# A logits bank that holds one place of the key tiles for four heads, instead of four key tiles of one head

## The chip, the cores and the metric

The kernel runs on one core of a Trainium2 chip. Its time is the device time of one execution in microseconds (us), given as the median of three runs.

## What is computed

Two blocks over an input `x` of 8 batches, 1024 tokens and 256 features, in fp32. The part that matters is the attention of the first block, with 16 heads of 16 features and a relative position term:

```
x = L0_attn_x
logits = einsum('bhqd,bhkd->bhqk', q, k) + einsum('bhqd,qkd->bhqk', q, embK[idx])
w = softmax(logits, axis=-1)
out = einsum('bhqk,bhkd->bhqd', w, v) + einsum('bhqk,qkd->bhqd', w, embV[idx])
x = x + layernorm(out @ Wo.T + bo)
x = x + layernorm(layernorm(x) @ ternary(W).T * alpha + bias)
```

`idx` is the distance of key and query, clipped to 64 on either side. So the relative term differs from token to token only in a band around the diagonal, and is one constant per side elsewhere.

## The kernel before

**Steps.** The heads are in two groups of 8 and the queries in tiles of 128. That makes 8 x 2 x 8 = 128 steps `s`. A step is worked in two halves (`blk` 0 and 1, four heads each), and four steps make a quad, of which there are 32. The 8 key tiles of a query tile are sorted by `near_first`: places 0 and 1 are the two that the band touches (left and right), places 2 to 7 lie further round.

**The stages of a step.** `row_max` forms the scores of one head in the two PSUM banks of `scores` (L748 on TensorE); VectorE adds the band to the first bank and takes its maximum (L1044), then takes the maximum of the second bank (L1047). TensorE may write the next head's first bank after L1044 has read it, and its second bank after L1047. `max_rows` turns the maxima. `weights` forms the logits transposed, in one of `NLOG` = 2 banks `logitsT` (L770); for places 0 and 1 a second matmul in transpose mode adds the band (L775). ScalarE takes the exponential of the whole bank into SBUF (L1251). `weighted` multiplies by the values into `oacc` (L800). `merge` joins left and right weights on VectorE (L1069). Once in a quad `relative` multiplies the merged weights of four steps by the table of the relative values (L812), and `relative_sum` and `out_norm` finish them. The projections of the next batch and the "tail" (output projection, the layer norms, the ternary matmul; L864) are spread between these.

**The banks of `weights`.** A half has eight banks: four of kind X (places 0 to 3), one for each head, and four of kind Y (places 4 to 7), one for each head. So an X bank takes six matmuls, four L770 and two L775, and a Y bank four L770. The bank that is used alternates, and each waits until ScalarE is done with the bank two before it: `pe.wait_ge(exp_ready, block + 1 - NLOG)`.

**Where the weights lie.** `wxr` in SBUF holds places 0 and 1 of four steps (`wx`) and, behind them, places 2 and 3 of one half (`wr`); one ACTIVATE writes to both. `wy` holds places 4 to 7 of one half.

**Order.** Each engine runs its stages in an order that a table of slots sets (`timetable`, with `LAG`): the X banks of a half stand at `o + 0.4 * j`, the Y banks at `o + 1.7 + 0.4 * j`, the heads of `row_max` at every 0.87 slots, `weighted` X at `o + 2.3`. The engines meet only at semaphores.

Below, a bank is called by its step's number in the quad, its half and its place in the half's eight banks: "X0 to X3" and "Y0 to Y3".

Of the kernel before, what the change touches and what calls it, by code (L numbers as in the profile page):

```python
# [14 lines left out]
P = 128  # L15
B, S, H = 8, 1024, 256
NH, D, MRP = 16, 16, 64
VOCAB = 2 * MRP + 1
T = S // P
G = 2  # L20
HG = NH // G
# [7 lines left out]
FAR = MAXROW + 2  # L29
ROWS = FAR + 3  # L30
# [3 lines left out]
WIN = 2 * P  # L34
# [3 lines left out]
QUAD = 4  # L38
# [3 lines left out]
QRING, BRING, VRING = 5, 7, 3  # L42
HB = HG // 2
# [266 lines left out]
def build(nc, a, out):  # L310
    with ExitStack() as ctx:
        def sb(name, shape, dt=F32):
            return ctx.enter_context(nc.sbuf_tensor(name, shape, dt))
# [12 lines left out]
        ident = sb("ident", [P, P])  # L326
# [14 lines left out]
        qs = [sb(f"qs{i}", [ROWS, HG, P], BF16) for i in range(QRING)]  # L341
        vs = [sb(f"vs{i}", [P, 2, T, HG, VW]) for i in range(VRING)]
        bands = sb("bands", [P, (BRING * HB + 1) * WIN])
        band = [bands[:, i * HB * WIN:(i + 1) * HB * WIN].rearrange("p (h c) -> p h c", h=HB) for i in range(BRING)]
        zeros = bands[:, BRING * HB * WIN:]
        praw = sb("praw", [P, HG, WIN])
        embk6, partmask = praw[0:SPLIT, 0, 0:VOCAB], praw[0:SPLIT, 0, VOCAB:VOCAB + 3]
        wxr = sb("wxr", [P, (QUAD * HG + 4) * WIN])
        wx = wxr[:, 0:QUAD * HG * WIN].rearrange("p (i h c) -> p i h c", i=QUAD, h=HG)
        wr = wxr[:, QUAD * HG * WIN:].rearrange("p (j c) -> p j c", j=4)  # L350
        wy = sb("wy", [P, 4, 512])
        junk = sb("junk", [P, 2, WIN], BF16)
        maxes = [sb(f"maxes{i}", [P, HG, 2]) for i in range(2)]
# [6 lines left out]
        x0 = wxr[:, 0:T * H].rearrange("p (t h) -> p t h", t=T)  # L360
        xc = sb("xc", [P, CHUNK, H])
        xnT = sb("xnT", [P, 2, CT])
        qf = sb("qf", [P, G, CT])
# [24 lines left out]
        value = counts(orders)  # L388
# [32 lines left out]
        def n(signal, stage, *k):  # L421
            return value.get((signal, stage) + k, 0)
# [35 lines left out]
        def wait_x1(eng, b, t):  # L458
            if last_tile(b, t):
                eng.wait_ge(x1_ended, t - T + QUAD + 1)  # L460
            else:
                eng.wait_ge(x1_ready, b * T + t + 1)

        def wait_praw(eng):

# [209 lines left out]
        def tensor_program(e):  # L675
            pe, order = Engine(e), orders["PE"]
            for stage, k in order:
# [80 lines left out]
                elif stage == "weights":  # L758
                    s, h, kind = k
                    m_, t = s // T, tile_of(s)  # L760
                    i, kk = s % QRING, ks[m_ % 2]
                    tiles = near_first(t)[0:4] if kind == "X" else near_first(t)[4:]
                    block = n("logits_ready", "weights", s, h, kind) - 1
                    lt = logitsT[block % NLOG]
                    pe.wait_ge(nm_in[s % 2], 32 * (s // 2 + 1))
                    pe.wait_ge(exp_ready, block + 1 - NLOG)
                    for c, kt in enumerate(tiles):
                        near = kind == "X" and c < 2
                        depth = ROWS if is_right(t, kt) else FAR
                        mm = e.matmul(lt[:, c * P:(c + 1) * P], kk[0:depth, h, kt * P:(kt + 1) * P], qs[i][0:depth, h, :],  # L770
                                      start=True, stop=not near, skip_group_check=True)
                        if near:
                            v = 2 * s + h // HB
                            pe.wait_ge(band_in[v % BRING], band_loads(v))
                            mm = e.matmul(lt[:, c * P:(c + 1) * P], band[v % BRING][:, h % HB, c * P:(c + 1) * P], ident[:],  # L775
                                          start=False, stop=True, is_transpose=True, skip_group_check=True)
                    mm.then_inc(logits_ready, 1)
                elif stage == "weighted":
# [11 lines left out]
                    for c, kt in enumerate(tiles):  # L790
                        for q0, q1, right in value_sides(t, kt):
                            for j in range(4):
                                h = 4 * blk + j
                                if kind == "Y":
                                    src = wy[:, j, c * P + q0:c * P + q1]
                                elif c < 2:
                                    src = wx[:, s % QUAD, h, c * P + q0:c * P + q1]
                                else:
                                    src = wr[:, j, (c - 2) * P + q0:(c - 2) * P + q1]
                                mm = e.matmul(oacc[32 * j:32 * j + VW, o0 + q0:o0 + q1], vs[m_ % VRING][:, int(right), kt, h, :],  # L800
                                              src, start=first and c == 0, stop=True, skip_group_check=True)
                    mm.then_inc(pvX if kind == "X" else pvY, 1)
                elif stage == "relative":
# [4 lines left out]
                    for i in range(8 * part + 2 * piece, 8 * part + 2 * piece + 2):  # L808
                        o0 = i % 8 * QUAD * HG * 2
                        for j in range(4):  # L810
                            q = 32 * j + 2 * i
                            mm = e.matmul(m[32 * j:32 * j + 32, o0:o0 + QUAD * HG * 2],  # L812
                                          reltab[:, 126 - q:128 - q, :].rearrange("p n d -> p (n d)"),
                                          wx[:, :, :, P + q:P + q + 2], start=True, stop=True, skip_group_check=True)
                    if piece == 3:
                        mm.then_inc(rel_summed, 1)
                elif stage == "relative_sum":
# [92 lines left out]
        def vector_program(e):  # L910
# [45 lines left out]
            for stage, k in order:  # L956
# [104 lines left out]
                    e.tensor_tensor(nm[:, 1], m[0:HG, 0:P], nm[:, 0], ALU.subtract).then_inc(nm_ready, 1)  # L1061
                elif stage == "merge":
                    s, blk = k
                    left, right = (wx[:, s % QUAD, HB * blk:HB * blk + HB, x:x + P] for x in (0, P))
# [111 lines left out]
        def scalar_program(e):  # L1176
            act, order = Engine(e), orders["ACT"]
            for stage, k in order:
# [41 lines left out]
                elif stage == "band_raw":  # L1220
                    s, blk = k
                    act.wait_ge(raw_summed, n("raw_summed", "band_raw", s, blk))
                    v = 2 * s + blk
                    if s:
                        act.wait_ge(band_out[(v - 2) % 4], 16 * ((v - 2) // 4 + 1))
                    dst, src = praw[:, HB * blk:HB * blk + HB, :], m[:].rearrange("p (h c) -> p h c", h=HB)
                    e.activation(dst[:, :, 0:P], src, ACT.Copy)  # L1227
                    e.activation(dst[:, :, P:WIN], src[:, :, P - 1:P].broadcast_to([P, HB, P]), ACT.Copy).then_inc(praw_ready, 1)  # L1228
                elif stage == "weights":
                    s, h, kind = k  # L1230
                    block = n("logits_ready", "weights", s, h, kind) - 1
                    lt = logitsT[block % NLOG]
                    act.wait_ge(logits_ready, block + 1)
                    done = pvX if kind == "X" else pvY
                    if kind == "X":
                        if s >= QUAD:
                            act.wait_ge(rel_summed, 2 * (s // QUAD))
                            act.wait_ge(pvX, value["pvX", s - QUAD, h // 4])
                        at_ = (s % QUAD * HG + h) * WIN
                        dst = bass.AP(wxr, at_, [[(QUAD * HG + 4) * WIN, P], [(QUAD * HG + h % 4) * WIN - at_, 2], [1, WIN]])  # L1240
                        src = lt[:].rearrange("p (a c) -> p a c", a=2)
                    else:
                        dst, src = wy[:, h % 4, :], lt[:]
                        for c in (1, 3):
                            act.wait_ge(q_out[0][c], 96)
                            act.wait_ge(k_out[0][c], 96)
# [144 lines left out]
```

## Time and profile before

| | |
|---|---|
| time, median of 3 runs | 2637.41 us (2637.28 to 2637.48) |
| span of the profiled execution | 2629.6 us (first to last instruction) |
| the runs' median less that span | 7.8 us |
| TensorE busy | 2474.5 us, 94% |
| VectorE busy | 2044.9 us, 78% |
| ScalarE busy | 1552.6 us, 59% |
| GpSimd busy | 926.1 us, 35% |
| mean granted TensorE clock | 0.984 |

The profiled execution's time outside of its span is not recorded; the three runs agree within 0.2 us, so the median stands for it. TensorE's busy share counts each matmul from its start to its modelled end, and neighbours overlap. The pace at which it gets through its work is therefore read from the starts in the timeline, and a wait from the note in brackets behind a row. The middle of the kernel is periodic: a quad takes about 79 us.

### The profile page before, as it was taken

The page shows a single profiled execution, that of the slowest core. Times are in us where ns is not written, and L with a number is a line of the kernel's source. Part 1 is how long each engine was busy: PE and PEld are TensorE (multiplying, and loading weights), DVE is VectorE, ACT ScalarE, POOL GpSimd, SP SyncE. Part 2 cuts the span into 40 slices and gives each one's busy share as a digit, 9 for nine tenths or more (in the row PEclk, how much of TensorE's full clock was granted, in tenths as well). Part 3 has the DMA queues.
Part 4 walks back from the last instruction along what each step waited for, and adds up shares of the span by engine and source line. Part 5 has one row for each costly group of instructions (what it writes and reads, how often), then busy time and mean ns, then how long its engine had stood idle before and what let it go on. Part 6 is the DMA issues. An engine that isn't in the chain of part 4 may idle for free.

```text
span 2629.6 us, 99990 instructions
## 1 busy us (share of the span) xinstructions
PE 2474.5 (94%) x41858; PEld 1901.8 (72%) x41858; DVE 2044.9 (78%) x5306; ACT 1552.6 (59%) x2993; POOL 926.1 (35%) x2211
## 2 busy tenths in 40 slices
PE   5699999999999999999999999999999999999995
PEld 3377777777777777777777777777777777777774
DVE  5577678876888768876788767987678876887786
ACT  3366666565666556665566665566666565666652
POOL 3002534335332443424434253433434334342014
PEclk9699999999999999999999999999999999999997
DMA  6655664557545565455645566445654556545410
GB/s 167 205 159 152 186 174 130 153 156 201 152 149 153 156 183 157 138 161 171 184 137 156 153 179 185 134 140 161 200 165 131 152 155 195 163 137 169 128 54 30
DMA packets 605183, 408.07 MB, mean 155 GB/s; under 512 B 149563, under 2 KB 604475, under 8 KB 604603
## 3 DMA queue, kind: packets, MB, share of 16 engines
q1 hardware_dynamic: 604730, 401.67, 52.8%
q8 instruction: 329, 5.39, 0.9%
q14 instruction: 124, 1.01, 0.1%
HBM read 205.95 MB, written 194.92 MB: 152 GB/s over the span
## 4 chain that ended last, share of the span: by engine, by line
PE 64%; DVE 23%; issue 6%; ACT 2%; SPq 2%; DMA 1%; POOL 1%; DVEq 0%; ACTq 0%; POOLq 0%
PE oacc L800 15%; PE logitsT L770 14%; PE scores L748 12%; DVE maxes L1047 9%; DVE junk L1044 8%; PE logitsT L775 7%; PE misc L705 4%; PE misc L864 3%; ACT wxr L1251 2%; PE misc L722 2%; DVE stats L922 2%; PE misc L825 2%; PE misc L812 1%; PE misc L732 1%; PE misc L850 1%
## 5 line engine op out<-in xcount | busy, mean ns | idle before, releaser
L770 PE MATMUL logitsT<-qs,ks 98*128 98x128 bf16 (+1 forms) x8192 | 977.5, 220 | 15.9 <-ACT wxr L1251 7.9
L1044 DVE CUSTOM_DVE_ANT_1 junk<-scores,bands 128x512 bf16<-128x512 f32 x988 | 678.2, 686 | 338.8 <-PE scores L748 295.3
L1251 ACT ACTIVATE wxr<-logitsT 128x512 f32<-128x512 f32 x1024 | 587.9, 603 | 453.4 <-PE logitsT L770 356.0
L770 PEld LDWEIGHTS logitsT<-qs,ks 98*128 98x128 bf16 (+1 forms) x8192 | 669.1, 99 | 192.0 <-issue 58.1
L1251 ACT ACTIVATE wy<-logitsT 128x512 f32<-128x512 f32 x1024 | 587.3, 597 | 307.5 <-PE logitsT L770 295.2
L748 PE MATMUL scores<-ks,qs 96*128 96x256 bf16 (+6 forms) x3712 | 686.8, 288 | 83.8 <-DVE maxes L1047 38.4
L1047 DVE TENSOR_REDUCE maxes<-scores 128x1 f32<-128x512 f32 x1024 | 701.3, 685 | 1.5 <-PE scores L748 1.5
L748 PEld LDWEIGHTS scores<-ks,qs 96*128 96x128 bf16 (+1 forms) x3712 | 285.1, 98 | 261.8 <-DVE maxes L1047 133.8
L775 PE MATMUL logitsT<-ident,bands 128*128 128x128 f32 x2048 | 463.3, 278 | 0.0
L1280 POOL TENSOR_SCALAR rs<-rs 128x1 int32<-128x1 int32 (+1 forms) x217 | 47.7, 220 | 897.3 <-DVE rs L927 888.2
L775 PEld LDWEIGHTS logitsT<-ident,bands 128*128 128x128 f32 x2048 | 291.7, 142 | 43.5
L1285 POOL TENSOR_SCALAR rs<-rs 128x1 f32<-128x1 f32 x744 | 274.1, 371 | 64.9
L800 PE MATMUL oacc<-wy,vs 128*17 128x128 f32 (+1 forms) x9216 | 274.1, 262 | 0.7 <-ACT wy L1251 0.7
L800 PE MATMUL oacc<-wxr,vs 128*17 128x128 f32 (+1 forms) x9216 | 274.1, 262 | 0.0
L800 PEld LDWEIGHTS oacc<-wy,vs 128*17 128x17 f32 x9216 | 205.7, 97 | 39.5 <-issue 19.9
L800 PEld LDWEIGHTS oacc<-wxr,vs 128*17 128x17 f32 x9216 | 205.7, 97 | 35.6 <-issue 13.6
L1290 POOL TENSOR_SCALAR rs<-rs 128x1 f32<-128x1 f32 x744 | 207.6, 282 | 66.1
L1227 ACT ACTIVATE praw<-misc 128x512 f32<-128x512 f32 x256 | 153.4, 599 | 44.3 <-DMA bs<-praw 39.9
L1069 DVE COPY_PREDICATED wxr<-later,wxr 128x512 f32<-128x512 int32 x224 | 172.2, 769 | 8.2 <-PE oacc L800 8.2
L1228 ACT ACTIVATE praw<-misc 128x512 f32<-128x512 f32 x256 | 156.4, 611 | 0.0
L812 PE MATMUL misc<-wxr,reltab 128*32 128x64 f32 x4096 | 102.7, 242 | 0.0
L732 PE MATMUL misc<-bandtab,qs 96*128 96x128 bf16 x1024 | 100.2, 220 | 0.2
(141 smaller groups left out, 2433.9 us busy)
## 6 DMA issues: line engine op xcount, KB each, us to landing
bs<-praw SPq DMA_DIRECT2D x256, 512.0 KB, 4.3
bands<-bs SPq DMA_DIRECT2D x224, 512.0 KB, 4.6
ks<-kd SPq DMA_DIRECT2D x64, 384.0 KB, 4.4
qs<-qd SPq DMA_DIRECT2D x112, 192.0 KB
bands<-bs SPq DMA_DIRECT2D x128, 128.0 KB, 3.3
qd<-qparts SPq DMA_DIRECT2D x60, 192.0 KB, 2.9
kd<-kparts SPq DMA_DIRECT2D x60, 192.0 KB, 2.6
qd<-qparts SPq DMA_DIRECT2D x60, 128.0 KB, 2.6
```

What stands on the lines that cost most here:

```text
L748: mm = e.matmul(scores[:, c:c + length], qs[i][0:depth, h, :], kk[0:depth, h, key:key + length], start=True, stop=True, skip_group_check=True)
L770: mm = e.matmul(lt[:, c * P:(c + 1) * P], kk[0:depth, h, kt * P:(kt + 1) * P], qs[i][0:depth, h, :], start=True, stop=not near, skip_group ...
L775: mm = e.matmul(lt[:, c * P:(c + 1) * P], band[v % BRING][:, h % HB, c * P:(c + 1) * P], ident[:], start=False, stop=True, is_transpose=Tr ...
L800: mm = e.matmul(oacc[32 * j:32 * j + VW, o0 + q0:o0 + q1], vs[m_ % VRING][:, int(right), kt, h, :], src, start=first and c == 0, stop=True ...
L1044: e.tensor_tensor_reduce(junk[:], scores[:, 0:512].rearrange("p (a c) -> p a c", a=2), banded, 1.0, LOWEST, ALU.add, ALU.max, mx[:, h, 0:1 ...
L1047: e.tensor_reduce(mx[:, h, 1:2], scores[:, 512:S], AX.X, ALU.max).then_inc(row_maxed, 1)
L1069: e.copy_predicated(right, mask.bitcast(I32), left).then_inc(merged, 1)
L1227: e.activation(dst[:, :, 0:P], src, ACT.Copy)
L1228: e.activation(dst[:, :, P:WIN], src[:, :, P - 1:P].broadcast_to([P, HB, P]), ACT.Copy).then_inc(praw_ready, 1)
L1251: e.activation(dst, src, ACT.Exp).then_inc(exp_ready, 1)
L1285: op = e.tensor_scalar(rs[k][:, 3, x:x + 1], rs[k][:, 2, x:x + 1], rs[k][:, 0, x:x + 1], rs[k][:, 2, x:x + 1], ALU.mult, ALU.mult)
L1290: op = e.tensor_scalar(rs[k][:, 2, x:x + 1], rs[k][:, 3, x:x + 1], 1.5, rs[k][:, 2, x:x + 1], ALU.add, ALU.mult)
```

## The change

The same eight banks of a half are filled in another way. Bank `c` now holds place `c` of the key tiles for the half's four heads, instead of four places for one head. So X0 takes four L770 and four L775 (left near tile), X1 the same (right near tile), and X2, X3 and Y0 to Y3 four L770 each. The weights go to other buffers: X1 to `wm`, which keeps four steps, since `relative` reads only the merged right side; X0 to one of two buffers `wl`; X2 and X3 to `wr`; the Y banks to `wy`. The waits of ScalarE before it writes follow the buffers. The table of slots, and with it the order of the stages on every engine, stays as it is, as do `merge`, `weighted` and `relative` but for where they read.

```diff
-        wxr = sb("wxr", [P, (QUAD * HG + 4) * WIN])
-        wx = wxr[:, 0:QUAD * HG * WIN].rearrange("p (i h c) -> p i h c", i=QUAD, h=HG)
-        wr = wxr[:, QUAD * HG * WIN:].rearrange("p (j c) -> p j c", j=4)
+        wm = sb("wm", [P, QUAD, HG, P])
+        wl = [sb(f"wl{i}", [P, 512]) for i in range(2)]
+        wr = sb("wr", [P, 2, 512])
...
+        def wx_of(s, blk, c):
+            if c == 1:
+                return wm[:, s % QUAD, HB * blk:HB * blk + HB, :].rearrange("p h q -> p (h q)")
+            return wl[(2 * s + blk) % 2][:] if c == 0 else wr[:, c - 2, :] if c < 4 else wy[:, c - 4, :]
...
-                    tiles = near_first(t)[0:4] if kind == "X" else near_first(t)[4:]
+                    blk, c = h // HB, h % HB + (0 if kind == "X" else 4)
+                    kt = near_first(t)[c]
+                    near = c < 2
+                    depth = ROWS if is_right(t, kt) else FAR
...
-                    for c, kt in enumerate(tiles):
-                        near = kind == "X" and c < 2
-                        depth = ROWS if is_right(t, kt) else FAR
-                        mm = e.matmul(lt[:, c * P:(c + 1) * P], kk[0:depth, h, kt * P:(kt + 1) * P], qs[i][0:depth, h, :],
-                                      start=True, stop=not near, skip_group_check=True)
+                    for j in range(HB):
+                        mm = e.matmul(lt[:, j * P:(j + 1) * P], kk[0:depth, HB * blk + j, kt * P:(kt + 1) * P],
+                                      qs[i][0:depth, HB * blk + j, :], start=True, stop=not near, skip_group_check=True)
...
-                                          wx[:, :, :, P + q:P + q + 2], start=True, stop=True, skip_group_check=True)
+                                          wm[:, :, :, q:q + 2], start=True, stop=True, skip_group_check=True)
...
-                    if kind == "X":
-                        if s >= QUAD:
-                            act.wait_ge(rel_summed, 2 * (s // QUAD))
-                            act.wait_ge(pvX, value["pvX", s - QUAD, h // 4])
...
-                    if h >= 4:
-                        act.wait_ge(done, value["pv" + kind, s, 0])
-                    elif s:
-                        act.wait_ge(done, value["pv" + kind, s - 1, 1])
+                    if c == 0 and v >= 2:
+                        act.wait_ge(merged, n("merged", "merge", *divmod(v - 2, 2)))
+                    elif c == 1 and s >= QUAD:
+                        act.wait_ge(rel_summed, 2 * (s // QUAD))
+                    elif c > 1 and v:
+                        act.wait_ge(done, value["pv" + kind, (v - 1) // 2, (v - 1) % 2])
```

What this does to TensorE's order is seen at two places. The first is the first half of step 46 (the third step of a quad), on TensorE, from X2 to Y1 with what stands between. Before, lines L770 and L775 are the logits and the band, L850 turns rows for the tail and L756 the maxima:

```order
L770 MATMUL logitsT0<-qs1,ks1 128x128
L775 MATMUL logitsT0<-ident,bands 128x128
L770 MATMUL logitsT0<-qs1,ks1 128x128
L775 MATMUL logitsT0<-ident,bands 128x128
L770 MATMUL logitsT0<-qs1,ks1 128x128 x2
L770 MATMUL logitsT1<-qs1,ks1 128x128
L775 MATMUL logitsT1<-ident,bands 128x128
L770 MATMUL logitsT1<-qs1,ks1 128x128
L775 MATMUL logitsT1<-ident,bands 128x128
L770 MATMUL logitsT1<-qs1,ks1 128x128 x2
L770 MATMUL logitsT0<-qs1,ks1 128x128 x4
L850 MATMUL misc0<-ident,zbuf0 128x128 x2
```

And the same piece with the change, where the logits are L778, the tail's turn L852 and that of the maxima L762:

```order
L754 MATMUL scores<-ks1,qs2 128x512
L778 MATMUL logitsT0<-qs1,ks1 128x128 x4
L778 MATMUL logitsT1<-qs1,ks1 128x128 x4
L778 MATMUL logitsT0<-qs1,ks1 128x128 x4
L852 MATMUL misc0<-ident,zbuf0 128x128 x2
L762 MATMUL misc2<-ident,negmax1 8x128
L778 MATMUL logitsT1<-qs1,ks1 128x128 x4
```

The four L775 of X2 and X3 have gone to X0 and X1, which stand earlier, so that three banks of four matmuls each now follow one another. The second place is the first half of step 48 (the first of a quad), on TensorE, from X1 over the scores of one head to X2. Before:

```order
L770 MATMUL logitsT1<-qs3,ks0 128x128
L775 MATMUL logitsT1<-ident,bands 128x128
L770 MATMUL logitsT1<-qs3,ks0 128x128
L775 MATMUL logitsT1<-ident,bands 128x128
L770 MATMUL logitsT1<-qs3,ks0 128x128 x2
L748 MATMUL scores<-ks0,qs4 128x256 x2
L748 MATMUL scores<-ks0,qs4 128x384
L748 MATMUL scores<-ks0,qs4 128x128
L770 MATMUL logitsT0<-qs3,ks0 128x128
L775 MATMUL logitsT0<-ident,bands 128x128
```

And with the change, where L754 is the scores:

```order
L778 MATMUL logitsT1<-qs3,ks0 128x128
L782 MATMUL logitsT1<-ident,bands 128x128
L778 MATMUL logitsT1<-qs3,ks0 128x128
L782 MATMUL logitsT1<-ident,bands 128x128
L778 MATMUL logitsT1<-qs3,ks0 128x128
L782 MATMUL logitsT1<-ident,bands 128x128
L778 MATMUL logitsT1<-qs3,ks0 128x128
L782 MATMUL logitsT1<-ident,bands 128x128
L754 MATMUL scores<-ks0,qs4 128x256 x2
L754 MATMUL scores<-ks0,qs4 128x384
L754 MATMUL scores<-ks0,qs4 128x128
L778 MATMUL logitsT0<-qs3,ks0 128x128 x4
```

Here two more L775 stand ahead of the scores and none is left in the bank behind them.

## Rows read from the trace of the kernel before

**Rows 1.** The page: span, busy time, and the chain that ended last by engine.

```profile
span 2629.6 us, 99990 instructions
PE 2474.5 (94%) x41858; PEld 1901.8 (72%) x41858; DVE 2044.9 (78%) x5306; ACT 1552.6 (59%) x2993; POOL 926.1 (35%) x2211
PE 64%; DVE 23%; issue 6%; ACT 2%; SPq 2%; DMA 1%; POOL 1%; DVEq 0%; ACTq 0%; POOLq 0%
```

**Rows 2.** The page's costliest groups: busy us, mean ns, idle before and releaser.

```profile
L770 PE MATMUL logitsT<-qs,ks 98*128 98x128 bf16 (+1 forms) x8192 | 977.5, 220 | 15.9 <-ACT wxr L1251 7.9
...
L1251 ACT ACTIVATE wxr<-logitsT 128x512 f32<-128x512 f32 x1024 | 587.9, 603 | 453.4 <-PE logitsT L770 356.0
...
L775 PE MATMUL logitsT<-ident,bands 128*128 128x128 f32 x2048 | 463.3, 278 | 0.0
...
L1069 DVE COPY_PREDICATED wxr<-later,wxr 128x512 f32<-128x512 int32 x224 | 172.2, 769 | 8.2 <-PE oacc L800 8.2
...
L812 PE MATMUL misc<-wxr,reltab 128*32 128x64 f32 x4096 | 102.7, 242 | 0.0
```

**Rows 3.** The waits: engine, line, awaited, us in total, times, longest.

```profile
DVE junk L1044 <- PE scores L748: 310.2, 386, 3.8
...
PEld scores L748 <- DVE maxes L1047: 133.8, 328, 0.8
...
PEld logitsT L770 <- ACT wxr L1251: 51.2, 222, 0.6
```

**Rows 4.** Timeline of TensorE in step 46, first half, X2 to Y0.

```profile
1004.17 0.22 PE L770 MATMUL logitsT<-qs,ks 98*128 98x128 bf16 x1
...
1004.52 0.33 PE L770 MATMUL logitsT<-qs,ks 98*128 98x128 bf16 x3
...
1004.98 0.28 PE L770 MATMUL logitsT<-qs,ks 98*128 98x128 bf16 x2
1005.49 0.40 PE L770 MATMUL logitsT<-qs,ks 98*128 98x128 bf16 x4 [0.23 <-ACT wxr L1251]
1005.72 0.39 PE L850 MATMUL misc<-ident,zbuf 128*128 128x128 f32 x2
```

**Rows 5.** Timeline of ScalarE there: the exponentials of X2 and X3.

```profile
1004.83 1.09 ACT L1251 ACTIVATE wxr<-logitsT 128x512 f32<-128x512 f32 x2 [1.34 <-PE logitsT L770]
```

**Rows 6.** Timeline of TensorE in step 45, first half: the start of Y0.

```profile
988.78 0.40 PE L770 MATMUL logitsT<-qs,ks 98*128 98x128 bf16 x4 [0.23 <-ACT wxr L1251]
```

**Rows 7.** Timeline of TensorE in step 47, first half: scores, X2, X3, scores, tail.

```profile
1018.38 0.60 PE L748 MATMUL scores<-ks,qs 96*128 96x256 bf16 x3
...
1019.74 0.82 PE L748 MATMUL scores<-ks,qs 96*128 96x256 bf16 x3
1020.39 0.38 PE L864 MATMUL misc<-wo,rowsT 128*128 128x256 f32 x1
```

**Rows 8.** Timeline of VectorE there: the maxima of the first head.

```profile
1018.81 0.69 DVE L1044 CUSTOM_DVE_ANT_1 junk<-scores,bands 128x512 bf16<-128x512 f32 x1 [0.81 <-PE scores L748]
...
1019.42 0.69 DVE L1047 TENSOR_REDUCE maxes<-scores 128x1 f32<-128x512 f32 x1
```

**Rows 9.** Timeline of TensorE in step 48, first half: scores between X1 and X2.

```profile
1042.64 0.38 PE L748 MATMUL scores<-ks,qs 96*128 96x256 bf16 x2
1043.19 0.39 PE L748 MATMUL scores<-ks,qs 101*128 101x384 bf16 x2 [0.16 <-DVE maxes L1047]
1043.42 0.22 PE L770 MATMUL logitsT<-qs,ks 98*128 98x128 bf16 x1
```

**Rows 10.** Timeline of VectorE there.

```profile
1043.05 0.68 DVE L1078 TENSOR_TENSOR relout<-misc,relmask 128x512 f32<-128x512 f32 x1
1043.64 0.68 DVE L1044 CUSTOM_DVE_ANT_1 junk<-scores,bands 128x512 bf16<-128x512 f32 x1
```

**Rows 11.** Timeline of TensorE in step 48, second half: scores behind Y0.

```profile
1055.69 0.86 PE L748 MATMUL scores<-ks,qs 96*128 96x256 bf16 x4
1056.39 0.39 PE L770 MATMUL logitsT<-qs,ks 101*128 101x128 bf16 x4
```

More of the change, by code:

```diff
@@ L359, in build @@
         attn = [sb("attn0", [P, T, P]), sb("attn1", [P, QUAD, P])]
-        x0 = wxr[:, 0:T * H].rearrange("p (t h) -> p t h", t=T)
+        x0 = wm[:].rearrange("p i h q -> p (i h q)")[:, 0:T * H].rearrange("p (t h) -> p t h", t=T)
         xc = sb("xc", [P, CHUNK, H])
@@ L761, in tensor_program @@
                     i, kk = s % QRING, ks[m_ % 2]
-                    tiles = near_first(t)[0:4] if kind == "X" else near_first(t)[4:]
+                    blk, c = h // HB, h % HB + (0 if kind == "X" else 4)
+                    kt = near_first(t)[c]
+                    near = c < 2
+                    depth = ROWS if is_right(t, kt) else FAR
                     block = n("logits_ready", "weights", s, h, kind) - 1
                     lt = logitsT[block % NLOG]
+                    v = 2 * s + blk
                     pe.wait_ge(nm_in[s % 2], 32 * (s // 2 + 1))
                     pe.wait_ge(exp_ready, block + 1 - NLOG)
-                    for c, kt in enumerate(tiles):
-                        near = kind == "X" and c < 2
-                        depth = ROWS if is_right(t, kt) else FAR
-                        mm = e.matmul(lt[:, c * P:(c + 1) * P], kk[0:depth, h, kt * P:(kt + 1) * P], qs[i][0:depth, h, :],
-                                      start=True, stop=not near, skip_group_check=True)
+                    for j in range(HB):
+                        mm = e.matmul(lt[:, j * P:(j + 1) * P], kk[0:depth, HB * blk + j, kt * P:(kt + 1) * P],
+                                      qs[i][0:depth, HB * blk + j, :], start=True, stop=not near, skip_group_check=True)
                         if near:
-                            v = 2 * s + h // HB
                             pe.wait_ge(band_in[v % BRING], band_loads(v))
-                            mm = e.matmul(lt[:, c * P:(c + 1) * P], band[v % BRING][:, h % HB, c * P:(c + 1) * P], ident[:],
+                            mm = e.matmul(lt[:, j * P:(j + 1) * P], band[v % BRING][:, j, c * P:(c + 1) * P], ident[:],
                                           start=False, stop=True, is_transpose=True, skip_group_check=True)
@@ L793, in tensor_program @@
                                 h = 4 * blk + j
[L794 to L799, printed above, removed]
+                                src = wx_of(s, blk, c if kind == "X" else c + 4)[:, j * P + q0:j * P + q1]
                                 mm = e.matmul(oacc[32 * j:32 * j + VW, o0 + q0:o0 + q1], vs[m_ % VRING][:, int(right), kt, h, :],
@@ L1063, in vector_program @@
                     s, blk = k
-                    left, right = (wx[:, s % QUAD, HB * blk:HB * blk + HB, x:x + P] for x in (0, P))
+                    left, right = (wx_of(s, blk, x).rearrange("p (h q) -> p h q", h=HB) for x in range(2))
                     mask = later[:].rearrange("p (h q) -> p h q", h=1).broadcast_to([P, HB, P])
@@ L1234, in scalar_program @@
                     done = pvX if kind == "X" else pvY
-                    if kind == "X":
-                        if s >= QUAD:
-                            act.wait_ge(rel_summed, 2 * (s // QUAD))
-                            act.wait_ge(pvX, value["pvX", s - QUAD, h // 4])
[L1239 to L1246, printed above, removed]
-                    if h >= 4:
-                        act.wait_ge(done, value["pv" + kind, s, 0])
-                    elif s:
-                        act.wait_ge(done, value["pv" + kind, s - 1, 1])
+                    blk, c = h // HB, h % HB + (0 if kind == "X" else 4)
+                    v = 2 * s + blk
+                    if c == 0 and v >= 2:
[4 more added lines that the diff above has]
+                        act.wait_ge(done, value["pv" + kind, (v - 1) // 2, (v - 1) % 2])
+                    if kind == "Y":
+                        for c_ in (1, 3):
+                            act.wait_ge(q_out[0][c_], 96)
+                            act.wait_ge(k_out[0][c_], 96)
+                    dst, src = wx_of(s, blk, c), lt[:]
                     e.activation(dst, src, ACT.Exp).then_inc(exp_ready, 1)
```

## Prediction

> **What bounds the kernel now.** I read the page first. TensorE is busy for 94% of the span and carries 64% of the chain that ended last; VectorE carries 23%, ScalarE 2% [rows 1]. So TensorE sets the pace, with VectorE taking over for stretches. The view of waits says how: TensorE waits for VectorE's maxima (133.8 us in 328 places) and for ScalarE's exponentials (51.2 us in 222), and VectorE waits for scores 310.2 us in 386 [rows 3]. Each engine runs a fixed order and hands over through two banks of `scores` or two of `logitsT`. The reader is to see that no engine is short of throughput; time is lost where work of uneven length meets a ring of two. The timelines then show what decides a wait.
>
> *How fast a bank fills.* In step 46, X2 starts at 1004.17. Its third tile starts at 1004.52: two tiles with band took 0.35 us, 0.175 each [rows 4]. A bank without band, Y0, takes 1005.49 to 1005.72, 0.23 us, 0.057 a tile [rows 4]. So an X bank of before takes 2 x 0.175 + 2 x 0.057 = 0.46, a bank of four near tiles will take 0.70 and one of four far tiles 0.23. The band costs 0.12 a tile.
>
> *How fast ScalarE gives it back.* The two exponentials that start at 1004.83 take 1.09 together and one alone 0.60 on average, so ScalarE takes a new one every 0.49 us [rows 2, 5]. The last matmul of X2 starts near 1004.58, its exponential at 1004.83 and ends at 1005.43, and Y0, which needs that bank, starts at 1005.49 [rows 4, 5]: 0.91 us from the last matmul's start to the reuse of the bank. TensorE doesn't wait only if what it has between, the bank in between and whatever the order puts there, covers that.
>
> **The change, part by part.**
>
> *Matmuls: nothing.* The count of L770 and L775 stays, 8192 and 2048 [rows 2]. Each L775 still stands behind an L770 of its own tile, so the alternation between the two kinds doesn't change either. ScalarE: 2048 exponentials of 512 columns as before, 0.60 each; that each now writes one run instead of two I cost at nothing, since two runs of 256 in place of one cannot be worth more than a few of the 603 ns [rows 2]; at a bound of 10 ns either way, 1024 of them are 10 us on an engine that idles 41% [rows 1], of which a tenth at most would lie in the 0.91 us turn-around that TensorE waits for. The `merge` (769 ns, 224 times) reads and writes runs of 128 elements before and after; nothing, and if its time fell by 5%, 9 us would come off an engine with 22% idle [rows 1, 2]. `relative` reads pairs of elements as before, at half the distance; no row shows such a read at two distances, so between nothing and, should it be slower or faster by a tenth, 10 us of the 103 us of L812 either way; I take nothing, and keep 5 us of it for the range [rows 2].
>
> *Waits of ScalarE: nothing.* X0 now waits for a merge of a whole step before, X1 for `relative`, and only X2 for `weighted`. All these come later or for older work than before. Ahead of a quad X0 is even free of the wait for `relative`, but TensorE is itself at work on `relative` then. What is queued behind X1's wait is X2's exponential; TensorE needs X1's bank again only at X3.
>
> *The fill of the banks: this is the change.* Against before, TensorE is 0.23 late after X0, 0.47 after X1, 0.23 after X2 and level again after X3. If nobody waited for anybody, the sum would be nil. But a wait that is cut or grown does not come back. I went along one quad (steps 45 to 48) with this lateness and asked at each place where the timeline shows a wait who is late.
>
> 1. *Step 45, first half.* X2, X3, Y0 stand together; Y0 waits for the exponential of X2 and has 0.23 of idle time already [rows 6]. X2 now ends 0.23 later than before while X3 is 0.23 shorter, so the start of Y0 moves by the 0.23 that X2 moved. Loss 0.22 us. The waits of logits on ScalarE come 222 times, 7 in a quad [rows 3], so this is in most quads; I take 25 of 32: +5.5 us.
> 2. *Step 46, first half.* The same at 1005.49 [rows 4]. But here Y1 waits too, for X3, which ends when it did; its exponential starts at most 0.49 behind that of X2, as before. About 0.12 of the 0.22 is taken back there, so +0.10 in 32 quads: +3.2 us.
> 3. *Step 47, first half.* A head's scores stand behind X1 (1018.38), the next head's behind X3 (1019.74) [rows 7]. VectorE waits 0.81 for the first, works on it from 1018.81 to 1020.11 [rows 8], and TensorE waits for that at its second bank: the row takes 0.65 to the next start where its twin takes 0.44 [rows 7, 8]. With the change the first head comes 0.44 late, the second would be level, but VectorE is not done. Loss 0.44, in the quads where nothing else stands between; I take 24: +10.6 us.
> 4. *Step 48, first half.* A gain. The scores behind X1 (1042.64) need their second bank from VectorE, which is busy up to 1043.05, where its next instruction starts, and take 0.78 us instead of 0.44 [rows 9, 10]. The 0.47 of lateness is eaten by that wait of 0.34, and X2 and X3 are short afterwards. VectorE takes this head at 1043.64 only [rows 10], so it isn't delayed. 31 quads by -0.34: -10.5 us.
> 5. *Step 48, second half.* The scores behind Y0 take 0.70 to the next start (1055.69 to 1056.39) against 0.44: they wait for VectorE [rows 11]. The head before stands between X2 and X3 and comes 0.23 later. The lead of place 4 is partly given back: 24 quads by +0.22: +5.3 us.
>
> In the second halves of steps 45 and 46 I find gain and loss of about 0.2 each and count nothing. Sum: 5.5 + 3.2 + 10.6 - 10.5 + 5.3 = **+14 us**. The span of 2629.6 becomes 2644; with the 7.8 us around it, and against the median of 2637.4, **2651.5 us**.
>
> A rule to weigh here. First the rows: with two banks in turn, TensorE still idles 0.23 before Y0 [rows 4]. The Trainium skill (Perfetto Trace Analysis, Matmuls under Optimizing Tensor Performance) says that independent groups should rotate through PSUM banks, so that one group's evacuation overlaps the next one's matmuls. By that rule alone both kernels, which rotate through the same two banks, would hide ScalarE alike, and the sum would be nil, 2637.4 us. The row agrees only in part.
>
> **The rivals.**
>
> *A. The waits eat it: no change.* VectorE idles for 310.2 us before the scores [rows 3], so lateness may be swallowed at the next place where TensorE waits for it. For: 328 such waits, ten in a quad. Against: at place 3 TensorE is what VectorE waits for. Then 2637, within 5 us.
>
> *B. Faster.* The long banks X0 and X1 stand in front of the places where TensorE waits for VectorE or ScalarE anyway, and only X2, X3 get shorter. One place has this for certain, step 48 (-10.5 us); it decides if the 0.44 of place 3 is absorbed too, which takes only VectorE being behind at 1018.38 (there it idles 0.81 [rows 8]). Then -10.5 + 5.5 + 3.2 = -2, and with another such gain of 0.34 in each quad, where TensorE's 133.8 us of waits for L1047 [rows 3] hold ten candidates a quad, -12: 2625 us.
>
> *C. Much slower.* Each far bank runs into ScalarE. Per half X3 and Y0 lose 0.22 wherever less than 0.22 of slack is left behind the 0.91. If in all 256 halves one did: 256 x 0.22 = 56 us, 2694 us. Against: most halves have scores (0.44) or `weighted` (1.0) between these banks.
>
> **How the numbers follow.** The measurement tells 0.2%, 5.3 us, from nothing. My forecast (2643 to 2672): 0.57. A: 0.14. B: 0.22. C: 0.07. The likeliest case has 2651.5. Its parts could each be off by the number of quads I chose, which gives 2643 if half of places 1, 3 and 5 hold, and 2665 if the gain of place 4 is lost. The range 2628 to 2670 leaves out the further part of B and C. Faster 0.22, same 0.14, slower 0.64.
>
> **What the profile after would show.** L770 and L775 with the same counts, and busy times within 1%. The exponential and the merge unchanged. Waits of logits for ScalarE up by 10 us or more, now at X3 and Y0 and none at X1. Waits of scores for L1047 changed at steps 47 (up) and 48 (down, to 0.1 a quad). The quad's period up from 79 by about 0.4 us. I am wrong if the waits of scores for VectorE fall by more than those for ScalarE rise, or if the fill of a near bank isn't 0.70.

## The result, and the profile after

The changed kernel takes **2665.7 us** (median of 4 runs, 2665.2 to 2670.3) against 2637.4 for the kernel before: +28.4 us, a ratio of 1.0114 (95% interval 1.0100 to 1.0129). It is slower, as forecast, and lies inside the range, but by twice the forecast +14.

The page of the changed kernel, its span, busy time and chain by engine, answers to [rows 1]:

```profile
span 2663.8 us, 100275 instructions
PE 2492.2 (94%) x41858; PEld 1899.4 (71%) x41858; DVE 2049.4 (77%) x5306; ACT 1567.0 (59%) x2993; POOL 926.1 (35%) x2211
...
PE 65%; DVE 23%; issue 5%; ACT 2%; SPq 2%; POOL 1%; DMA 1%; DVEq 0%; ACTq 0%; POOLq 0%
```

The same number of matmuls, exponentials and merges, and the same shares of the chain within a point: TensorE still sets the pace. This run took 2665.6 us, 1.8 more than its span, and so does every later run on record. With that, the profiled execution of the kernel before took about 2631.4 us (an estimate), some 6 less than its median, and of the 7.8 us in the table of before only some 2 lie outside the span. So the two spans are 34.2 us apart where the medians are 28.4. The costliest groups of the page answer to [rows 2]:

```profile
L778 PE MATMUL logitsT<-qs,ks 98*128 98x128 bf16 (+1 forms) x8192 | 937.6, 220 | 31.6 <-ACT wr L1250 19.4
...
L1250 ACT ACTIVATE wr<-logitsT 128x512 f32<-128x512 f32 x512 | 290.8, 596 | 173.5 <-PE logitsT L778 160.9
...
L782 PE MATMUL logitsT<-ident,bands 128*128 128x128 f32 x2048 | 402.4, 278 | 0.0
...
L1071 DVE COPY_PREDICATED wm<-later,wl 128x512 f32<-128x512 int32 x224 | 171.7, 766 | 6.6 <-PE oacc L802 6.6
```

One matmul, one exponential and one merge last what they lasted. The idle time ahead of the logits has doubled, 15.9 to 31.6. And the waits, which answer to [rows 3]:

```profile
DVE junk L1046 <- PE scores L754: 347.9, 404, 3.6
...
PEld scores L754 <- DVE maxes L1049: 126.2, 296, 0.8
...
PEld logitsT L778 <- ACT wr L1250: 72.8, 212, 0.6
PEld logitsT L778 <- ACT wm L1250: 12.5, 61, 0.5
```

TensorE now waits 72.8 us at Y0 and Y1 for the far banks' exponentials, and 12.5 at X3 for that of X1. Together that is 85.3 where all X banks had 51.2 before. It waits 7.6 less for L1049, and VectorE waits 37.7 more for scores.

To see where the time went I took the start of every matmul in both traces and added up, from start to start, each half of a step over the 30 middle quads. These sums are worked out from all matmul rows, so no single row shows them. "Measured" is after minus before:

| half (step in the quad) | forecast, us | measured, us |
|---|---|---|
| 1st step, first half (48: place 4) | -10.5 | -2.6 |
| 1st step, second half (place 5) | +5.3 | +1.9 |
| 2nd step, first half (45: place 1) | +5.5 | +5.0 |
| 2nd step, second half | 0 | +0.2 |
| 3rd step, first half (46: place 2) | +3.2 | +6.5 |
| 3rd step, second half | 0 | +4.6 |
| 4th step, first half (47: place 3) | +10.6 | +10.3 |
| 4th step, second half | 0 | +6.3 |

Behind the last half, one stage that forms the next band (L738) loses a wait and gives back 3.2; the tail and the other stages, which I did not assign to halves, add about 1.5 (the tail's turn in the third step's first half alone adds 2.4, so that half, from its X0 to the next, is 8.8 longer). Together that is some 30 us in 30 quads, within the interval of the ratio (26 to 34 us). The mean quad between steps 8 and 120 went from 78.5 to 79.5 us.

Four places as rows. First, TensorE and ScalarE of the changed kernel in step 46, first half, X2 to Y0, which answer to [rows 4, 5]:

```profile
1017.42 0.61 PE L778 MATMUL logitsT<-qs,ks 98*128 98x128 bf16 x8
1018.50 0.40 PE L778 MATMUL logitsT<-qs,ks 98*128 98x128 bf16 x4 [0.47 <-ACT wr L1250]
1018.74 0.39 PE L852 MATMUL misc<-ident,zbuf 128*128 128x128 f32 x2
```

```profile
1017.85 1.08 ACT L1250 ACTIVATE wr<-logitsT 128x512 f32<-128x512 f32 x2 [1.10 <-PE logitsT L778]
```

X2 and X3 are eight matmuls in 0.45 us, then nothing until the exponential of X2 has ended at 1018.45. The last matmul of X2 starts near 1017.59, so the turn-around is again 0.91. The idle note went from 0.23 to 0.47.

A place that I had costed at nothing: TensorE and then ScalarE in step 46, second half, from X2 over the scores to Y0 and Y1:

```profile
1024.48 0.62 PE L778 MATMUL logitsT<-qs,ks 98*128 98x128 bf16 x8
1024.94 0.60 PE L754 MATMUL scores<-ks,qs 96*128 96x256 bf16 x3
1025.57 0.89 PE L778 MATMUL logitsT<-qs,ks 98*128 98x128 bf16 x8
```

```profile
1024.91 1.08 ACT L1250 ACTIVATE wr<-logitsT 128x512 f32<-128x512 f32 x2 [0.65 <-PE logitsT L778]
```

Before, on TensorE at the same place:

```profile
1011.91 0.60 PE L748 MATMUL scores<-ks,qs 96*128 96x256 bf16 x3
1012.35 0.84 PE L770 MATMUL logitsT<-qs,ks 98*128 98x128 bf16 x8
```

The scores take 0.44 to the next start before and 0.63 now: Y0 stands ready and waits for the exponential of X2, which ends at 1025.51. Before, X3 (0.46) and the scores (0.44) covered the 0.91 almost exactly: from X2's last matmul (1011.40) to Y0 it was 0.95. Now X3 gives only 0.23. No bracket marks this wait, since the row of scores still runs.

Third, step 47, first half, TensorE behind X1, which answers to [rows 7]:

```profile
1032.11 0.60 PE L754 MATMUL scores<-ks,qs 96*128 96x256 bf16 x3
1032.55 0.81 PE L778 MATMUL logitsT<-qs,ks 101*128 101x128 bf16 x8
1033.29 0.39 PE L754 MATMUL scores<-ks,qs 96*128 96x256 bf16 x2
1033.89 0.39 PE L754 MATMUL scores<-ks,qs 101*128 101x512 bf16 x1 [0.21 <-DVE maxes L1049]
1034.11 0.60 PE L866 MATMUL misc<-wo,rowsT 128*128 128x256 f32 x2
```

Between the two scores TensorE now has two short banks, 0.74 with their waits in place of 0.45. Then it waits for L1049: 0.82 for a stage that takes 0.44. By the starts, X3 stands 0.41 behind X2, which fills in 0.23; the 0.18 between is a wait for the exponential of X1, 5.5 us in 30 quads. And step 48, the gain, TensorE behind X1, which answers to [rows 9]:

```profile
1056.72 0.61 PE L754 MATMUL scores<-ks,qs 96*128 96x256 bf16 x4
1057.17 0.39 PE L778 MATMUL logitsT<-qs,ks 101*128 101x128 bf16 x4
```

The wait of 0.34 is gone here, as forecast. But the mean over the quads fell only from 0.60 to 0.45: by the starts of the kernel before, these scores took 0.78 to 0.80 in 14 of the 30 quads and 0.44 or 0.45, without a wait, in the other 16.

### The profile page after: what moved, and what is told of

Its sections match the earlier page's. It is cut to its first block, busy times and chain, and to the rows that moved or that the text cites. A ratio compares the mean times of both kernels' runs of the same rounds, so it can differ in the third digit from the quotient of the medians.

```text
span 2663.8 us, 100275 instructions
## 1 busy us (share of the span) xinstructions
PE 2492.2 (94%) x41858; PEld 1899.4 (71%) x41858; DVE 2049.4 (77%) x5306; ACT 1567.0 (59%) x2993; POOL 926.1 (35%) x2211
## 4 chain that ended last, share of the span: by engine, by line
PE 65%; DVE 23%; issue 5%; ACT 2%; SPq 2%; POOL 1%; DMA 1%; DVEq 0%; ACTq 0%; POOLq 0%
PE oacc L802 15%; PE logitsT L778 13%; PE scores L754 12%; DVE maxes L1049 9%; DVE junk L1046 8%; PE logitsT L782 8%; PE misc L866 4%; PE misc L711 4%; PE misc L814 2%; ACT wr L1250 2%; PE misc L728 2%; PE misc L827 2%; DVE stats L924 2%; PE misc L738 1%; SPq L517 1%
## 5 line engine op out<-in xcount | busy, mean ns | idle before, releaser
L778 PE MATMUL logitsT<-qs,ks 98*128 98x128 bf16 (+1 forms) x8192 | 937.6, 220 | 31.6 <-ACT wr L1250 19.4
L778 PEld LDWEIGHTS logitsT<-qs,ks 98*128 98x128 bf16 (+1 forms) x8192 | 608.0, 98 | 231.4 <-ACT wr L1250 72.8
L754 PE MATMUL scores<-ks,qs 96*128 96x256 bf16 (+6 forms) x3712 | 681.5, 288 | 82.1 <-DVE maxes L1049 38.5
L1049 DVE TENSOR_REDUCE maxes<-scores 128x1 f32<-128x512 f32 x1024 | 701.4, 685 | 1.9 <-PE scores L754 1.9
L754 PEld LDWEIGHTS scores<-ks,qs 96*128 96x128 bf16 (+1 forms) x3712 | 293.1, 98 | 255.0 <-DVE maxes L1049 126.2
L782 PE MATMUL logitsT<-ident,bands 128*128 128x128 f32 x2048 | 402.4, 278 | 0.0
L1250 ACT ACTIVATE wr<-logitsT 128x512 f32<-128x512 f32 x512 | 290.8, 596 | 173.5 <-PE logitsT L778 160.9
L1284 POOL TENSOR_SCALAR rs<-rs 128x1 f32<-128x1 f32 x744 | 275.0, 372 | 64.9
L1250 ACT ACTIVATE wl<-logitsT 128x512 f32<-128x512 f32 x256 | 156.8, 613 | 162.4 <-PE logitsT L782 162.3
L1250 ACT ACTIVATE wm<-logitsT 128x512 f32<-128x512 f32 x256 | 154.5, 604 | 120.8 <-PE logitsT L782 117.8
L1071 DVE COPY_PREDICATED wm<-later,wl 128x512 f32<-128x512 int32 x224 | 171.7, 766 | 6.6 <-PE oacc L802 6.6
L802 PE MATMUL oacc<-wr,vs 128*17 128x128 f32 (+1 forms) x4608 | 159.1, 261 | 0.0
L802 PEld LDWEIGHTS oacc<-wr,vs 128*17 128x17 f32 x4608 | 115.9, 98 | 0.0
```

The source lines that it names most:

```text
L754: mm = e.matmul(scores[:, c:c + length], qs[i][0:depth, h, :], kk[0:depth, h, key:key + length], start=True, stop=True, skip_group_check=True)
L778: mm = e.matmul(lt[:, j * P:(j + 1) * P], kk[0:depth, HB * blk + j, kt * P:(kt + 1) * P], qs[i][0:depth, HB * blk + j, :], start=True, sto ...
L782: mm = e.matmul(lt[:, j * P:(j + 1) * P], band[v % BRING][:, j, c * P:(c + 1) * P], ident[:], start=False, stop=True, is_transpose=True, s ...
L1049: e.tensor_reduce(mx[:, h, 1:2], scores[:, 512:S], AX.X, ALU.max).then_inc(row_maxed, 1)
L1071: e.copy_predicated(right, mask.bitcast(I32), left).then_inc(merged, 1)
L1284: op = e.tensor_scalar(rs[k][:, 3, x:x + 1], rs[k][:, 2, x:x + 1], rs[k][:, 0, x:x + 1], rs[k][:, 2, x:x + 1], ALU.mult, ALU.mult)
```

## The experiments

The theory U: nothing but the uneven fill of the banks costs time, in an order made for even ones. Rivals: S, the new buffers or ScalarE's new waits; D, only the scores that reach VectorE late; and that a ring of two logits banks is all of it.

| run | us | ratio to before, interval |
|---|---|---|
| new filling, old store | 2668.5 | 1.0130 (1.0116 to 1.0144) |
| places 0, 2, 1, 3 | 2659.1 | 1.0093 (1.0078 to 1.0109) |
| places 2, 3, 0, 1 | 2644.8 | 1.0040 (1.0027 to 1.0052) |
| places 2, 0, 3, 1 | 2637.4 | 1.0010 (1.0001 to 1.0019) |
| new store, even filling | 2634.2 | 0.9996 (0.9987 to 1.0004) |
| no band, before / changed | 2534.1 / 2529.7 | 0.9611 / 0.9597 |
| three banks, before / changed | 2643.9 / 2678.2 | 1.0043 (1.0029 to 1.0057) / 1.0165 (1.0146 to 1.0183) |
| scores moved, one place | 2668.5 | 1.0123 (1.0108 to 1.0137) |
| scores moved, both places | 2665.1 | 1.0117 (1.0103 to 1.0131) |
| the kernel before, scores moved | 2638.7 | 1.0015 (1.0006 to 1.0024) |

The ratios count, since single runs of the kernel before, taken beside these, lay between 2631.4 and 2638.5 us.

**New filling, old store.** The banks as changed, all buffers and waits as before:

```diff
-                        at_ = (s % QUAD * HG + h) * WIN
-                        dst = bass.AP(wxr, at_, [[(QUAD * HG + 4) * WIN, P], [(QUAD * HG + h % 4) * WIN - at_, 2], [1, WIN]])
-                        src = lt[:].rearrange("p (a c) -> p a c", a=2)
+                        c, hs = h % HB, slice(h // HB * HB, h // HB * HB + HB)
+                        dst = wx[:, s % QUAD, hs, c * P:(c + 1) * P] if c < 2 else wr[:, :, (c - 2) * P:(c - 1) * P]
+                        src = lt[:].rearrange("p (h q) -> p h q", h=HB)
```

> Banks filled as in the changed kernel (one place, four heads), but weights kept in the old buffers with the old waits of ScalarE. Theory U (the loss is the uneven fill of the banks in a fixed order): 2663 to 2668 us, like the changed kernel, with the same waits of TensorE for ScalarE. Rival S (the loss lies in the new buffers, in how ScalarE writes and VectorE and TensorE read them, or in the new waits): 2635 to 2642 us, like the kernel before. In between, by its share, if both.

1.0130, against 1.0114 for the change: the intervals overlap. Summed by halves over the 30 quads the loss runs -3.2, -1.4, 3.6, 3.9, 10.4, 15.0, 25.4, 31.6; in the changed kernel it runs -2.6, -0.7, 4.3, 4.5, 11.0, 15.6, 25.9, 32.2. Its waits for the X banks' exponentials are those of the changed kernel too, 85.2 us in 273 places against 85.3 (72.8 + 12.5) in 273:

```profile
PEld logitsT L772 <- ACT wxr L1252: 85.2, 273, 0.6
```

The store is not needed for the loss.

**New store, even filling.** The other half of the change alone: buffers `wl`, `wm`, `wr` (laid out in one tensor `wall`) and their waits, but each X bank holds one near and one far place of two heads.

```diff
+                    if kind == "Y":
+                        cells = [(c, j) for j in range(HB)]
+                    else:
+                        cells = [(c % 2 + 2 * a, c // 2 * 2 + b2) for a in range(2) for b2 in range(2)]
+                    for x_, (place, j) in enumerate(cells):
...
+                        dst = bass.AP(wall, a0, [[WALL, P], [a1 - a0, 2], [1, 256]])
```

> The changed kernel's buffers and waits, but each X bank holds two places of two heads, one near and one far: four logits matmuls and two band matmuls in each of the four, 0.46 us as before the change. ScalarE writes two runs of 256. Theory U: the time of the kernel before, within 5 us. Rival S: 2660 us or more. Rival W (ScalarE's new waits bring something of their own, hidden by the long banks): between, or faster than before by a few us.

0.9996: the kernel before, within 0.1%. Its waits, to be held against [rows 3]:

```profile
PEld scores L756 <- DVE maxes L1055: 133.8, 328, 0.8
...
PEld logitsT L784 <- ACT wall L1263: 51.3, 222, 0.6
```

These are the waits of before in number and sum, and no half of a quad differs by more than 0.5 us in 30. So the fill makes the whole loss and the store none; W, a gain by ScalarE's looser waits, isn't there either.

**No band matmuls, in both kernels.** The second matmul of a near tile is taken out (the relative term is missing from the weights):

```diff
-                            mm = e.matmul(lt[:, j * P:(j + 1) * P], band[v % BRING][:, j, c * P:(c + 1) * P], ident[:],
-                                          start=False, stop=True, is_transpose=True, skip_group_check=True)
```

> The kernel before, without the band matmuls of the logits (the relative term is left out of the weights; the scores keep it). Every bank then fills in 0.23 us. Alone it says what 2048 band matmuls cost: 0.12 us each is 240 us if TensorE were never kept waiting; since the banks then all run into ScalarE's turn-around, I expect 100 to 200 us less than before. It is the pair of the next run.

> The changed kernel, without the band matmuls of the logits in the same way. All banks fill in 0.23 us in both kernels, so nothing is uneven. Theory U: the same time as its pair within 5 us. Rival S (buffers, or ScalarE's waits): 25 to 30 us more than its pair. The old store was already as slow as the new one in this filling, so S could now only be something that the filling itself brings, such as the order of the operands.

2534.1 and 2529.7 us: with all banks equal, the changed kernel is no slower (4 us faster by the medians; the intervals 0.9596 to 0.9626 and 0.9584 to 0.9610 overlap). The 28 us need the band, whose 2048 matmuls give back only about 100 of the 240 us that they issue for.

**The order of the places.** Only the list of places changes:

```diff
+XPLACE = (0, 2, 1, 3)
...
-                    blk, c = h // HB, h % HB + (0 if kind == "X" else 4)
+                    blk, c = h // HB, XPLACE[h % HB] if kind == "X" else h % HB + 4
```

> The changed kernel with the X banks in the order of places 0, 2, 1, 3, so that a long bank (0.70 us) and a short one (0.23 us) alternate. Theory U, with the parts that I gave it: TensorE is 0.23 late after the first and third bank and level after the second and fourth. The late scores ahead of the third bank (step 47, 10.6 us) go away, so does the gain of step 48; the waits before Y0 stay. 2650 to 2660 us. Rival S: 2666 us, since the buffers are the same. Rival D (the loss is all in how late VectorE gets the scores): about 2640 us.

> The changed kernel with the X banks in the order of places 2, 3, 0, 1: the short banks first, the long ones last. Theory U: TensorE is ahead of the kernel before by 0.23 after the first bank and 0.47 after the second, 0.23 after the third; the long fourth bank covers the turn-around ahead of Y0, so the wait before Y0 (0.23 us idle before the change, more after it) goes to zero. Waits of logits for ScalarE fall below those of the kernel before; 2620 to 2640 us. Rival S: 2666 us. If short banks just move their waits to the front (X1 and X2 of each half), 2655 us or more.

> The changed kernel with the X banks in the order of places 2, 0, 3, 1: short, long, short, long. Theory U: TensorE is ahead by 0.23 after the first and third bank and level after the second and fourth. The long fourth bank covers the turn-around ahead of Y0, as in the order 2, 3, 0, 1 (2645 us), and no head's scores come 0.47 early or late, but the fourth bank now waits behind a short third one. 2635 to 2645 us. If the waits at the fourth bank cost more than those of far first at the third, 2650 us.

The first order gave 2659.1, within what U gave, and far from D's 2640. As TensorE is now at most 0.23 late behind X banks, never 0.47, the loss of the fourth step's first half is gone (-0.3 against +10.3 over 30 quads), as the parts said; the one of the second step's first half stays (+5.1). Far first gave 2644.8, slower than the 2620 to 2640 that I expected. The waits of logits for ScalarE didn't fall as expected either: 64.9 us in all, against 62.9 before (the 51.2 of [rows 3] and 11.7 for `wy`). Over the 30 quads Y0 waits 16 us less, but X1 and X2 wait 12 more and Y1 6 more; and the scores wait 180.0 us for VectorE over the kernel (L1050 and L1047) against 169.0 before. Far and near in turn gave 2637.4, as expected. Its waits for exponentials:

```profile
PEld logitsT L779 <- ACT wy L1251: 19.7, 62, 1.0
PEld logitsT L779 <- ACT wm L1251: 15.0, 66, 0.6
PEld logitsT L779 <- ACT wl L1251: 8.1, 40, 0.5
...
PEld logitsT L779 <- ACT wr L1251: 4.8, 25, 0.2
```

These are 47.6 us, below the 62.9 of the kernel before, and yet the kernel isn't faster. All of these kernels have the same store and the same work; the order of long and short banks alone moves them over 28 us. S falls, and D with it.

**Three banks of logits.** The third comes from the three shared banks, so that two are left for the other stages; every engine's order stays:

```diff
-NLOG, NMISC = 2, 3
+NLOG, NMISC = 3, 3
+BANKS = 2
...
-        misc = [ps(f"misc{i}", 512) for i in range(NMISC)]
+        misc = [ps(f"misc{i}", 512) for i in range(BANKS)]
```

> The kernel before with three banks of logits instead of two; the third is taken from the three shared banks of the other stages, which then wait more for one another, in the same order on every engine. It is the pair of the next run and has no time of its own that decides: it could be faster (the 75 us of waits for ScalarE go) or slower (the shared banks).

> The changed kernel with three banks of logits in the same way. If the loss is the ring of two banks of logits against ScalarE, the difference to the pair falls from 30 to 10 us or less. If it is the scores that come late or early at VectorE (place 3 of the prediction, a third of the loss), some 10 us or more stay. If it is neither, the whole 30 us stay.

The pair is 34 us apart by the medians, 29 by the two profiled executions, not 10. The waits of logits for ScalarE (62.9 us before, 95.0 changed) are gone in both but for 0.5, and the loss stays: it doesn't hang on the ring of two alone. Where it went is seen in TensorE's timeline of the changed kernel with three banks, step 46, first half, X2 to the turn of the maxima (L773):

```profile
1018.39 0.83 PE L789 MATMUL logitsT<-qs,ks 98*128 98x128 bf16 x12
1019.07 0.39 PE L863 MATMUL misc<-ident,zbuf 128*128 128x128 f32 x2
1020.36 0.27 PE L773 MATMUL misc<-ident,negmax 128*8 128x128 f32 x1 [0.91 <-DVE ybuf L1129]
```

X2, X3 and Y0 now run through in 0.68 us, but the maxima of the scores behind X1 are late, because X1 was. The row's note names L1129, a stage of the tail: it frees one of the two shared banks, and stands on VectorE right behind those maxima (L1066), from 1019.80. Over the kernel the wait of that turn for L1066 itself is 32.3 us in 40 places, against 15.6 in 33 in the pair without the change:

```profile
PEld misc L773 <- DVE negmax L1066: 32.3, 40, 1.1
```

At step 45, first half, it is the scores behind Y0 that take 6.0 us more over 30 quads than in the pair, by their starts. So the lateness comes out at VectorE where it no longer does at ScalarE. What is not shown is a third bank beside three shared ones: with two, the shared banks have waits of their own, as here.

**The scores moved.** One head's scores in front of X1 instead of behind it, in the fourth step of a quad; then also one ahead of the tail's matmul in the third:

```diff
-            at(m0 + 0.87 * h, "row_max", s, h)
+            at(m0 + 0.87 * h - {(0, 3): 0.08, (3, 7): 0.35}.get((s % QUAD, h), 0) * (s >= QUAD), "row_max", s, h)
...
-                at(o + 0.4 * j, "weights", s, 4 * blk + j, "X")
+                at(o + 0.4 * j + 0.05 * ((i, blk, j) == (3, 0, 1)), "weights", s, 4 * blk + j, "X")
```

The second line puts X1 behind the scores there; the run with one move has `(0, 3)` alone.

> The changed kernel with one head's scores (the fourth of the next step) moved from behind X1 to in front of it, in the fourth step of each quad: place 3 of the prediction, which lost 10 us. If those scores come too late to VectorE there, the next head's scores lose their wait of 0.39 us for L1049; against it X3 now stands only one short bank behind X1 and waits some 0.4 us more for ScalarE than now (0.2). Counted along the timeline this piece of TensorE's order takes 2.7 us in place of 3.0: 5 to 9 us less than the changed kernel, 2657 to 2662 us. Rival (the ring of logits alone costs the time at this place): no gain or a loss, 2666 us or more.

> As the run before, and in the third step of a quad the last head's scores moved ahead of the tail's output projection (L866), 0.9 us earlier, in the quads that have one there. With three banks of logits the loss at place 2 (0.4 us a quad) stayed and stood at the turn of the maxima, which waits for these scores. If that is what holds there, half of the quads gain up to 0.2 us each: 3 us less than the run before. If the ring alone holds: the same time as the run before.

> The kernel before with the same two moves of scores. There the bank X1 is 0.23 us shorter, so the moves should be worth less: 2632 to 2640 us, within 0.2% of the kernel before. A gain of 5 us or more would mean that the moves help for a reason of their own, and that the gain of the two runs before says little of the change.

The first expectation failed: 2668.5, no gain. TensorE in that piece of step 47:

```profile
1031.13 0.39 PE L778 MATMUL logitsT<-qs,ks 101*128 101x128 bf16 x4
1031.98 0.40 PE L778 MATMUL logitsT<-qs,ks 101*128 101x128 bf16 x4 [0.46 <-ACT wm L1250]
1032.22 0.60 PE L754 MATMUL scores<-ks,qs 96*128 96x256 bf16 x3
1032.66 0.81 PE L866 MATMUL misc<-wo,rowsT 128*128 128x256 f32 x3
```

The wait for L1049 is gone (0.44 for the scores), but X3 waits 0.62 for the exponential of X1, since only X2's four matmuls stand between. From the first scores or X1 to the end of the second scores it is 2.67 us here (1029.99 to 1032.66) and 2.71 in the changed kernel (1031.40 to 1034.11). I had counted the latter as 3.0, which double-counted a wait. By its own terms this run speaks for the rival, the ring alone; the three banks speak against that one alone. Both fit if two ways lead from X1 to what follows, one through ScalarE and the bank, one through the scores and VectorE, and are about equally long; that is inferred from the two runs, since none takes both ways away. The second move shortens the quad with a tail at step 46 from 8.47 to 8.36 us between X0 and the next half, but the totals of the two runs overlap: inconclusive by time. On the kernel before, the moves bring no gain but a loss of 0.15% (1.0015), and 5 us of it stand in the fourth step's first half.

## Why the prediction came out at half the size

The mechanism was right, and sizes of its terms failed: matmuls, exponentials and merges cost what they did; an X bank of near tiles fills in 0.71 us (1031.40 to 1032.11; 0.70 forecast) and a far one in 0.23; the time is lost where the short banks meet waits. The runs with one half of the change alone show that the fill is all of it. `relative` and `merge`, which I costed at nothing with bounds, cost nothing.

The steps that failed are terms of the sum:

- *Place 4, "31 quads by -0.34"*: sized from one quad's row and multiplied by all of them. The wait stood in 14 of 30 quads only, 0.16 in the mean, so -4.7 at the scores and -2.6 in the half. That is 8 us of the 14 that were missing. Place 5, which takes this lead back, was oversized in step with it, 5.3 against 1.9.
- *"In the second halves of steps 45 and 46 I find gain and loss of about 0.2 each and count nothing"*: true of 45 (+0.2), false of 46 (+4.6); that of step 47 (+6.3) I hadn't gone through. Both are Y0 behind scores behind a short X3. I had looked for brackets at waits, and before the change there was none here: 0.95 against 0.91. The slack was 0.04 (at step 46), which a wait list cannot show.
- *Place 2, "about 0.12 of the 0.22 is taken back"*: +6.5 instead of 3.2. In quads without the tail's turn the turn of the maxima stands there, and it needs the late scores.
- Places 1 and 3 measured 5.0 and 10.3 for 5.5 and 10.6. At place 3, though, I named one way (VectorE), and 5.5 us stand ahead of X3, for ScalarE. That the sum came out is in part luck; the moved scores brought nothing.

Errors of +8, -3, +11 and +3, less the 3.2 given back at the band stage, add up to 16, and the miss is 14. The bounds beside the likeliest case were added wrongly too: by its parts, half of places 1, 3 and 5 gives 2641 and not 2643, and place 4 lost gives 2662 and not 2665. My sign of an error "busy times within 1%" was no sign: L770 and L775 lost 4% and 13% of their busy time with the same pace. A line's busy time counts overlapping matmuls once: two L775 start 0.175 apart and last 0.278, so four in a row cover 0.80 us and two pairs 0.91.

Of the rivals, A and B assumed that a wait for VectorE swallows lateness. It does at step 48, in 14 of 30 quads, and hardly elsewhere. C had the other extreme; 28 us is half of its 56. The Trainium skill (Perfetto Trace Analysis, Matmuls under Optimizing Tensor Performance) says that groups should rotate through PSUM banks so that the evacuation of one overlaps the next one's matmuls. Taken alone, as in the prediction, that rule kept the time; the measurement is +28 us with the rotation unchanged, and with a third bank in it the difference stayed.

## What to carry to other kernels

In a fixed order over several engines, equal sums of work are not equal time: a long item followed by short ones makes everything behind the long one late, and the short ones cannot make it up, because the hand-over (0.91 us here) has a length of its own. Keep the items that share a ring equal, or try their order: here the long banks first cost 1.1%, last 0.4%, and short and long in turn 0.1%. And when you cost a shorter item, list the places with no slack, not only those with a wait. Adding a buffer or moving one stage may only show the second way of the same length. Here the even filling with the new store (2634.2 us, 0.9996) keeps the time of before with 24 KB per partition for the X weights instead of 36.

## What the runs showed that was not expected

- Taking 2048 band matmuls out, 0.12 us each or about 240 us of TensorE's issue time, saved 101 us (2634.9, the median of the kernel before in the runs beside it, less 2534.1). More than half of them lies in time in which TensorE would wait.
- The kernel before varies by more than its first three runs said: 2631.4 to 2638.5 us, 0.27%, where those lay within 0.2 us.
